# Row-maximum matmuls moved next to the exp matmuls, and the turning of the maxima moved forward

## The reference

```
qkv = x @ Wqkv + bqkv                       # 16 heads of 16 channels
att = softmax(causal(q @ k.T * 0.25))       # per head, 512 x 512
x   = layernorm(x + (att @ v) @ Wout + bout)
h   = silu(lin(x, w1)) * lin(x, w2)         # 256 -> 1024
h   = gelu(lin(h, h1)); h = gelu(lin(h, h2))  # 1024 -> 1024, twice
x   = layernorm(x + lin(h, w3))             # 1024 -> 256
```

## Time and profile before

| what | value |
|---|---|
| runs of the kernel | 2600.02, 2599.66 and 2599.02; median 2599.66 |
| span of the profiled execution | 2594.6, which is 5.1 less than the median of the runs; its own time is not listed apart |
| TensorE matmul busy | 2430.1, 94% |
| VectorE busy | 1282.1, 49% |
| ScalarE busy | 1344.6, 52% |
| GpSimd busy | 487.0, 19% |
| mean granted TensorE clock | 0.957 |

### The profile page before, as it was taken

The page is one execution under the profiler, slowest core; times in us unless marked ns, Lnnn a source line. Parts: engine busy times, 40 slices in busy tenths (PEclk is TensorE's granted clock), DMA queues, the critical chain, the costliest instruction groups (busy, mean ns, idle before and its releaser), DMA issues.

```text
span 2594.6 us, 54348 instructions
## 1 busy us (share of the span) xinstructions
PE 2430.1 (94%) x17318; PEld 1869.5 (72%) x17318; DVE 1282.1 (49%) x3896; ACT 1344.6 (52%) x3104; POOL 487.0 (19%) x894
## 2 busy tenths in 40 slices
...
PEclk7558999999999999999999999999999999999999
...
DMA packets 109426, 184.69 MB, mean 71 GB/s; under 512 B 20608, under 2 KB 38784, under 8 KB 108928
## 3 DMA queue, kind: packets, MB, share of 16 engines
...
...
## 4 chain that ended last, share of the span: by engine, by line
PE 76%; issue 7%; DVE 3%; POOL 3%; ACT 2%; POOLq 0%; DVEq 0%; ACTq 0%; DMA 0%; SPq 0%
PE ring L905 39%; PE ring L891 6%; PE pS L807 6%; PE ring L918 5%; PE pM L818 5%; PE pO L841 4%; PE ring L850 3%; PE ring L856 2%; PE ring L827 2%; PE ring L872 2%; POOL Xlo L483 2%; ACT probs L516 1%; POOL probs L477 1%; PE ring L880 1%; DVE pM L643 1%
## 5 line engine op out<-in xcount | busy, mean ns | idle before, releaser
L643 DVE CUSTOM_DVE_ANT_0 pM<-pM,mask 128x512 f32<-128x512 f32 (+3 forms) x1024 | 492.1, 510 | 537.4 <-PE pM L818 443.5
L516 ACT ACTIVATE probs<-pS 128x512 f32<-128x512 f32 (+3 forms) x1024 | 392.1, 434 | 304.0 <-PE pS L807 302.5
L905 PE MATMUL ring<-Xhi,H 128*128 128x256 f32 x2048 | 527.3, 297 | 19.9 <-POOL Xlo L483 13.1
L905 PE MATMUL ring<-Yhi,H 128*128 128x256 f32 x2048 | 532.7, 298 | 0.0
L905 PE MATMUL ring<-Ylo,H 128*128 128x256 f32 x2048 | 506.4, 285 | 0.0
L905 PE MATMUL ring<-Xlo,H 128*128 128x256 f32 x2048 | 497.5, 282 | 0.0
L477 POOL TENSOR_SCALAR_AFFINE_SELECT probs<-probs 128x256 f32<-128x256 f32 x512 | 211.2, 413 | 1340.0 <-ACT probs L516 1336.1
L905 PEld LDWEIGHTS ring<-Yhi,H 128*128 128x128 f32 x2048 | 396.4, 194 | 40.7 <-issue 21.4
L905 PEld LDWEIGHTS ring<-Xhi,H 128*128 128x128 f32 x2048 | 389.5, 190 | 50.1 <-ACT full_h L585 17.3
L905 PEld LDWEIGHTS ring<-Ylo,H 128*128 128x128 f32 x2048 | 397.3, 194 | 0.0
L905 PEld LDWEIGHTS ring<-Xlo,H 128*128 128x128 f32 x2048 | 390.6, 191 | 4.4 <-issue 3.3
...
## 6 DMA issues: line engine op xcount, KB each, us to landing
...
qk_d<-c_hi SPq DMA_DIRECT2D x128, 128.0 KB, 2.4
qk_d<-c_lo SPq DMA_DIRECT2D x128, 128.0 KB, 2.4
...
Oc<-Osb SPq DMA_DIRECT2D x256, 32.0 KB
...
```

Of the source, the lines that this page charges most:

```text
L516: nc.scalar.activation(probs[:, e % NP_BUF, s, 0:n], pS[:, s, 0:n], ACT.Exp, scale=SCALE).then_inc(exp_done, 1)
L643: nc.vector.tensor_tensor_reduce(pM[:, s, 0:n], pM[:, s, 0:n], mask[:, T - n:T], 1.0, NEG, ALU.add, ALU.max, mx[:, t, 2 * p + s:2 * p + s ...
L905: mm = nc.tensor.matmul(to, w, x_part, start=(k == 0 and m == 0), stop=(k == KB - 1 and m == 1))
```

## The change

Every exp step is now followed at once by one max step of the next group, in the order t = 3, 3, 2, 2, 1, 1, 0, 0. Before, four (stage 0 to 2) or two (stage 3) of the eight max steps of a stage stood in or just behind the exp stretch, and the others between the blocks of the hidden stretch. The neg_max step stands now behind h block 2, 0, 2 and 1 of the stages 0 to 3, instead of behind block 6, 4, 6 and 5. No step is added or removed.

```
-    def exps(g, between):
+    def exps(g, between, after_max):
...
                 add("exp", 0, g, kt, p)
+                add("max", after_max[0], after_max[1], TB - 1 - kt, p)
                 steps.extend(between.get(e, []))
...
-    m = maxes(0, 1)
     add("table", 0, "Exp", 0)
-    exps(0, {0: [("y", -1, (0,)), m[0]], 1: [("y", -1, (1,))], 2: [("h2", -2, (1, 0))],
-             4: [m[1]], 5: [m[2]], 6: [("h2", -2, (1, 1))], 7: [("ln1_stats", -1, ()), m[3]]})
+    exps(0, {0: [("y", -1, (0,))], 1: [("y", -1, (1,))], 2: [("h2", -2, (1, 0))], 6: [("h2", -2, (1, 1))],
+             7: [("ln1_stats", -1, ())]}, (0, 1))
     add("table", 0, "Gelu", 1)
-    hidden("h2", -2, 1, 0, 2, {2: [m[4]], 3: [m[5]], 4: [m[6]], 5: [m[7]], 6: [("neg_max", 0, (1,))]})
+    hidden("h2", -2, 1, 0, 2, {2: [("neg_max", 0, (1,))]})
...
     exps(1, gated(-1, 0, [(4, 0), (4, 1), (5, 2), (5, 3), (6, 4), (6, 5), (7, 6), (7, 7)],
-                  {0: [("qk", 0, (3,)), ("load_xT", 1, ()), m[0]], 1: [("x1_turn", -1, (0,))],
-                   2: [("x1_turn", -1, (1,))], 3: [m[1]], 5: [m[2]]}))
-    steps.append(m[3])
+                  {0: [("qk", 0, (3,)), ("load_xT", 1, ())], 1: [("x1_turn", -1, (0,))],
+                   2: [("x1_turn", -1, (1,))]}), (0, 2))
...
-    hidden("h1", -1, 0, 1, 0, {0: [m[4]], 1: [m[5]], 2: [m[6], ("load_x", 0, ())], 3: [m[7]],
-                               4: [("neg_max", 0, (2,))], 5: [("ln2_stats", -2, (1,))], 6: [("ln2", -2, (1,))]})
+    hidden("h1", -1, 0, 1, 0, {0: [("neg_max", 0, (2,))], 2: [("load_x", 0, ())],
+                               5: [("ln2_stats", -2, (1,))], 6: [("ln2", -2, (1,))]})
...
-    exps(2, {0: [("h2", -1, (0, 0))], 1: [m[0]], 2: [("h2", -1, (0, 1))], 3: [m[1]], 4: [m[2]], 6: [m[3]]})
+    exps(2, {0: [("h2", -1, (0, 0))], 2: [("h2", -1, (0, 1))]}, (0, 3))
     add("table", 0, "Gelu", 5)
-    hidden("h2", -1, 0, 2, 2, {2: [m[4]], 3: [m[5]], 4: [m[6]], 5: [m[7]], 6: [("neg_max", 0, (3,))]})
+    hidden("h2", -1, 0, 2, 2, {2: [("neg_max", 0, (3,))]})
...
-    exps(3, gated(-1, 1, [(0, 1), (1, 2), (2, 3), (3, 4), (4, 5), (5, 6), (6, 7)],
-                  {1: [m[0]]}))
-    steps.append(m[1])
+    exps(3, gated(-1, 1, [(0, 1), (1, 2), (2, 3), (3, 4), (4, 5), (5, 6), (6, 7)], {}), (1, 0))
...
-    hidden("h1", -1, 1, 3, 0, {-1: [("v", 1, (0,)), m[2]], 0: [m[3], ("v", 1, (1,)), ("den", 0, ())],
-                               1: [m[4], ("v", 1, (2,))], 2: [m[5], ("v", 1, (3,))], 3: [m[6], ("rec_save", 0, ())],
-                               4: [m[7], ("rec_load", 0, ())], 5: [("neg_max", 1, (0,)), ("qk", 1, (2,))],
+    hidden("h1", -1, 1, 3, 0, {-1: [("v", 1, (0,))], 0: [("v", 1, (1,)), ("den", 0, ())],
+                               1: [("v", 1, (2,)), ("neg_max", 1, (0,))], 2: [("v", 1, (3,))], 3: [("rec_save", 0, ())],
+                               4: [("rec_load", 0, ())], 5: [("qk", 1, (2,))],
                                6: [("ln2_stats", -1, (0,)), ("den_turn", 0, ())], 7: [("ln2", -1, (0,))]})
```

More of the change, by code:

```diff
@@ L102, in hidden @@
             add("h_rest", off, layer, half, j)
-    def maxes(off, g):
-        return [("max", off, (g, t, p)) for t in reversed(range(TB)) for p in range(PAIRS)]
     def gated(off, half, at, others):
@@ L114, in gated @@
         return between
-    m = maxes(0, 1)
     add("table", 0, "Exp", 0)
-    exps(0, {0: [("y", -1, (0,)), m[0]], 1: [("y", -1, (1,))], 2: [("h2", -2, (1, 0))],
-             4: [m[1]], 5: [m[2]], 6: [("h2", -2, (1, 1))], 7: [("ln1_stats", -1, ()), m[3]]})
+    exps(0, {0: [("y", -1, (0,))], 1: [("y", -1, (1,))], 2: [("h2", -2, (1, 0))], 6: [("h2", -2, (1, 1))],
+             7: [("ln1_stats", -1, ())]}, (0, 1))
     add("table", 0, "Gelu", 1)
-    hidden("h2", -2, 1, 0, 2, {2: [m[4]], 3: [m[5]], 4: [m[6]], 5: [m[7]], 6: [("neg_max", 0, (1,))]})
+    hidden("h2", -2, 1, 0, 2, {2: [("neg_max", 0, (1,))]})
     add("table", 0, "Exp", 2)
     add("ffn_out", -2, 1)
-    m = maxes(0, 2)
     add("ln1", -1)
     exps(1, gated(-1, 0, [(4, 0), (4, 1), (5, 2), (5, 3), (6, 4), (6, 5), (7, 6), (7, 7)],
-                  {0: [("qk", 0, (3,)), ("load_xT", 1, ()), m[0]], 1: [("x1_turn", -1, (0,))],
-                   2: [("x1_turn", -1, (1,))], 3: [m[1]], 5: [m[2]]}))
-    steps.append(m[3])
+                  {0: [("qk", 0, (3,)), ("load_xT", 1, ())], 1: [("x1_turn", -1, (0,))],
+                   2: [("x1_turn", -1, (1,))]}), (0, 2))
     add("ffn_hi", -1, 0, KB - 1)
     add("table", 0, "Gelu", 3)
-    hidden("h1", -1, 0, 1, 0, {0: [m[4]], 1: [m[5]], 2: [m[6], ("load_x", 0, ())], 3: [m[7]],
-                               4: [("neg_max", 0, (2,))], 5: [("ln2_stats", -2, (1,))], 6: [("ln2", -2, (1,))]})
-    m = maxes(0, 3)
+    hidden("h1", -1, 0, 1, 0, {0: [("neg_max", 0, (2,))], 2: [("load_x", 0, ())],
+                               5: [("ln2_stats", -2, (1,))], 6: [("ln2", -2, (1,))]})
     add("table", 0, "Exp", 4)
     add("qk", 1, 0)
-    exps(2, {0: [("h2", -1, (0, 0))], 1: [m[0]], 2: [("h2", -1, (0, 1))], 3: [m[1]], 4: [m[2]], 6: [m[3]]})
+    exps(2, {0: [("h2", -1, (0, 0))], 2: [("h2", -1, (0, 1))]}, (0, 3))
     add("table", 0, "Gelu", 5)
-    hidden("h2", -1, 0, 2, 2, {2: [m[4]], 3: [m[5]], 4: [m[6]], 5: [m[7]], 6: [("neg_max", 0, (3,))]})
+    hidden("h2", -1, 0, 2, 2, {2: [("neg_max", 0, (3,))]})
     add("table", 0, "Exp", 6)
```

1 line of the change is left out of this document (removed).

## The result

The changed kernel takes 2616.78 us, the median of 4 runs (2614.34 to 2621.18), beside 2599.34 for the kernel before (2598.98 to 2600.02). The ratio is 1.0079, with a 95% interval from 1.0067 to 1.0092: slower by 0.8%.

The account below looks back on a forecast made before the run. The prediction took TensorE's in-order stream to bound the kernel. From 2599.7 us, less 2.4 for the schedule (transfers included) and plus 23 for the clock, it forecast 2620 us, range 2572 to 2652.

Parts of the forecast that it names:

- The price of a pair in its places: A max pair costs 0.47 us alone in the hidden stretch, 0.18 behind an exp pair; four leaving save 1.8.
- Stage 1, +1.2: Stage 1: waits on VectorE's reductions make the first gu 2.95 us late; net 1.2 us longer, 15 times.
- Stage 2, +0.4: Stage 2: pv2 comes 1.55 us late; less 1.8 and with a ring-bank wait, 0.4 us longer, 15 times.
- Stage 0, -1.2: Stage 0: VectorE keeps up, exp stretch unchanged within 0.1; net 1.2 us shorter, 14 times.
- stage 3, -0.3: Stage 3: v0 comes 2.2 us late, six leaving pairs save 2.5; net 0.3 us shorter, 14 times.
- The ring wait, 0.6: Stages 0 and 2: with neg_max earlier, h block 3 waits 0.6 us for a ring bank.
- Transfers, -5.4: Earlier neg_max brings nm earlier: 2.4 us saved in iteration 1 and 3 in iteration 0, together 5.4.
- The clock, +23: Clock falls: most vanish in stage 0 (-12), new ones in stage 1 (+26) and stage 2 (+9); sum +23 us.
- Rival B: No new clock falls, stage 0's old ones gone, schedule as worked out: 2584 us, 0.6% faster; chance 0.28.
- Around the span, 5.1: Around the profiled execution's span of 2594.6 us lie 5.1, which makes the median of the runs, 2599.7.

Follow-up runs that it names:

- e6: e1 with stage 1's max pairs moved later, none in front of the two x1_turn and one behind each: 2624.9 us.
- e10: e1 with two stage 1 max pairs in front of the first gu, six behind it, and neg_max one h block later: 2640.1 us.
- e4: e1 with neg_max one h block later (behind block 3) in stages 0 and 2: 2596.1 us.
- e7: e3 and e4 in one: 2559.8 us.
- e1: The changed kernel with load_x of stage 1 in front of neg_max again: 2606.4 us.
- e5: e1 plus seven matmuls that nobody reads, behind the second exp pair of stage 1: 2593.7 us.
- e9: e8 with neg_max of stage 0 behind block 3 instead of block 2: 2554.6 us.
- e3: e1 with stage 1 laid out as in the kernel before: 2592.0 us.
- e8: e3 with stage 2 also laid out as in the kernel before, its neg_max included: 2559.5 us.

## Why the prediction came out as it did

The forecast was 2620 and the time is 2616.8, slower as forecast. Part of this is luck: the step that failed was too low by 15 us, and the clock was too high by 16.

**The price of a pair in its places.** Right in stage 1, where the hidden stretch got 1.9 shorter (1.8 predicted). In stage 2 it gave less: the pv steps came 1.57 late and the ring wait 0.45 to 0.58, and the stage grew by 0.9, so the four pairs gave back only about 1.2.

**Stage 1, +1.2.** Right, 1.24. x1_turn was predicted at + 5.0 (5.1) and gu at + 10.4 (10.39). The late x1_turn is not what holds gu, as e6 shows, where the turn is early and gu isn't. What holds it is the row of max pairs in front of it, each waiting for the reductions of the one before: with two pairs there (e10) gu is back at + 7.5.

**Stage 2, +0.4.** pv1 and pv2 came at + 11.05 and + 13.34, predicted + 11.0 and + 13.3. The stage's sum was mis-sized: +0.9 instead of +0.4.

**Stage 0, -1.2, and stage 3, -0.3.** They measured -1.5 and -0.5.

**The ring wait, 0.6.** Right in size: 0.58 in the trace, 0.45 to 0.5 by e4 and e7. The rows that it was read from give 1.81 - 1.31 = 0.5.

**Transfers, -5.4.** This is the step that failed. It looked only at nm's own transfers ("past no wait that matters") and not at load_x, which the diff leaves at block 2 while neg_max goes from block 4 to block 0. Of the two gains that it named, the 3 us for iteration 0 came in, and more (3.2 in front of stage 2, another 2.5 in stage 3). The 2.4 for iteration 1 didn't: the first exp pair of its stage 1 now waits 8.14 us for nm, where the earlier trace rows had 4.62, and the stage in front is only 0.2 us shorter. TensorE came to that wait earlier in the iteration, but nm landed hardly earlier in it.

```profile
229.19 0.79 PE L798 MATMUL pS<-Qs,Ks 64*128 64x512 f32 x2 [8.14 <-DMA Qs<-nm]
```

And x landed some 16 us later, GpSimd waited for it with the triangles behind, and stage 2 of iteration 0 grew by 15.5. The term is +9.9; e1 takes 11.4 back by putting load_x in front.

**The clock, +23.** The mechanism was right: e5 shows that the waits on VectorE at the start of stage 1 bring the falls, and 8 of 15 iterations had one (0.65 predicted). Its price was mis-sized: 1.75 instead of 2.7 in stage 1; two falls in stage 2 instead of six; and -10 instead of -12 in stage 0. The sum is +7. That a fall costs less in stage 1 fits a stretch in which VectorE was the bound as long as the clock was up: it is busy for 5.75 of 6.03 us before the fall and for 4.53 of 6.70 behind it. No run tests this by itself. Rival B, no new falls, did not happen: in e1's stage from 369.57 on the clock fell at about E0 + 6.1, and the longest wait of TensorE before it is 0.84 us.

```profile
369.57:375.60 6.03, 5.04 (x20) 2.31 (x19) 5.75 (x15) 3.10 (x6) 0.96 (x2) 1.00 0.01 2
375.70:382.40 6.70, 6.54 (x27) 3.34 (x27) 4.53 (x16) 3.05 (x8) 1.23 (x3) 0.50 0.70 192
```

The Trainium skill ("TensorE: Matmul & The Clock Gate", section "Why this matters for your kernels") asks that no long idle gaps be left between bursts of matmuls. This trace does not agree that this is enough: the fall above has no wait over 0.84 us in front of it.

**Around the span, 5.1.** For the changed kernel it was 1.7, and it is 1.6 to 1.8 for every execution of the study whose time and span both stand on record (2596.09 with 2594.4 for the kernel before, beside e9). By that, the profiled execution of before took about 2596.3, in the range of what that kernel took beside the experiments, and the other 3.4 of the 5.1 is the distance from it to the median of other executions. The predicted sum started from that median, so it is not touched. Why the kernel before took 2599.3 beside the result and 2596.1 to 2597.3 beside the experiments is open.

What stays open too is where falls come back when they are driven out of a stage. They moved from 1 to 2 (e3, e5) and to 0 (e3, e4), and few came back in e7 and e8 (six and four in the 12 iterations of the loop). No run tells what decides that.
